# Sliding-window attention inside a fused layer stack: two transfers moved to the next step, and the softmax mask written by ScalarE

## The chip, the cores and the metric

The kernel runs on one core of a Trainium2 chip. The metric is the device time of one execution in microseconds (us), the median over several executions. The engines are named as in the profile: PE (TensorE, with its weight loads shown apart as PEld), DVE (VectorE), ACT (ScalarE), POOL (GpSimd) and SP (SyncE, which here only issues DMAs). All five run their own instruction streams and meet at counting semaphores.

## The reference

The input is x of shape (4, 1024, 128) in fp32. First comes a causal multi-head attention with low-rank projections and a layer norm. Then, and this is where the change lies, six layers of local attention and feed-forward, each on the whole of x:

```
for i in range(6):
    x = attn_layer(shift_tokens(x), Wqkv[i], q_scale[i], k_scale[i], Wo[i]) + x
    x = ffn_layer(shift_tokens(x), ln_g[i], ln_b[i], W1[i], b1[i], W2[i], b2[i]) + x
```

`attn_layer` projects to q, k and v of 16 heads of 64, normalises q and k per head, rotates them, and attends in windows of 32 tokens: a query sees its own window and the one before it, 64 keys, from which `(it < jb) | (it > jb + w) | (jb == -1)` are masked ahead of the softmax. The third condition masks the missing window before the first one. A last layer norm ends the computation.

## The kernel before

The program is written out in full: no loops at run time. The six layers are the function `local_layers`. It works in steps; a step takes a pair of token tiles, 256 tokens of one batch element, so there are 6 x 4 x 4 = 96 pairs, and 3 more steps drain the pipeline. In one step four pairs are in flight: `now` is projected to q, k and v, `back1` (the pair before) goes through scores, softmax and probabilities times V, `back2` through the output projection, `back3` through the feed-forward block. Each engine has a `step(s)` function in which its work stands in a fixed order, written by hand; there is no planner. PSUM holds three banks `bank_d` and three `bank_a`, each set used in turn through a `Ring`, and two banks `scores` for the attention scores of one phase.

The attention of a pair runs in two phases `ph` (even and odd windows) and within each in two halves (eight heads each, one score bank each):

- PE, `score(s, pair, ph, half)` (L457): first the mask as a matrix product of a bf16 identity with the bf16 mask (L465), which opens the bank; then 64 small matmuls q x k (L473) that accumulate on it. Phase 1 has first to wait until DVE has read phase 0's scores (`scores_used`). Phase 0 is ahead of projections 6, 7 and 8 (L410), phase 1 behind them.
- DVE, `softmax_shift` (L740): row maximum (L748), then the subtraction of it into `prob` (L752), each one instruction of 128x1024.
- ACT, `exponentials` (L643): the exponential in place (L645), behind the copy of v's first chunk (`copy_v(s, 8)`, L621) and the squares of q and k (`square`, L609).
- DVE, `softmax_sum`: row sum and reciprocal (L761, L762), in DVE's order ahead of the second phase's row maximum. POOL, `normalise`: the product with the reciprocal (L949).
- PE, `transpose_probs` (L420), then `times_v` (L440): 256 small matmuls and as many weight loads a step.

In the odd phase `times_v` takes its rows from `v`, in the even phase from `v_back`, which holds the same rows moved down by 32 tokens, over partition borders. SP makes it (L352 to L360), as soon as v's last chunk is copied, by three DMAs: 96 partitions of v's both tiles (768 KB), 32 partitions from tile 0 to tile 1 (128 KB), and the last 32 tokens of the *other* v buffer, the pair before (128 KB). Other things to know: ACT loads its function table twice a step, before the exponentials and before the gelu gates (L664); projection 9 on PE waits until the gates of part A have been read from their bank; PE's own instructions are brought in by DMA as well (queue q8 in the profile).

Of the kernel before, what the change touches and what calls it, by code (L numbers as in the profile page):

```python
# [21 lines left out]
P = 128  # L22
# [110 lines left out]
def local_layers(nc, x_dram, x1_dram, w):  # L133
# [5 lines left out]
    with ExitStack() as ctx:  # L139
# [76 lines left out]
        xr_in = [sem(f"xr_in{i}") for i in range(2)]  # L216
        xs1_in = [sem(f"xs1_in{i}") for i in range(2)]
        v_back_in = [sem(f"v_back_in{i}") for i in range(2)]
        x1_out, x2_out = sem("x1_out"), sem("x2_out")
        wqk_in, wv_in, wo_in, wffn_in, qkrow_in = sem("wqk_in"), sem("wv_in"), sem("wo_in"), sem("wffn_in"), sem("qkrow_in")  # L220
        d_filled, d_free = sem("d_filled"), sem("d_free")
# [3 lines left out]
        qk_ready = sem("qk_ready")  # L225
        table_ready = sem("table_ready")
        scores_ready, scores_used = sem("scores_ready"), sem("scores_used")
        exp_done, inv_ready, prob_ready = sem("exp_done"), sem("inv_ready"), sem("prob_ready")
        xn_ready = sem("xn_ready")
        v_link = sem("v_link")  # L230
# [44 lines left out]
        def _(sp):  # L275
# [40 lines left out]
            def step(s):  # L316
                new, now, back1, back2, back3 = (s.pair(lag) for lag in (-1, 0, 1, 2, 3))

                if not isinstance(s.t, int) or s.t > MAX_LAG:
                    sp.wait_ge(x2_out, 16 * (s.t - MAX_LAG))  # L320
                if runs(now):


                    load_xs(new)
                if runs(back2):


                    sp.dma_start(xr[back2.par][:, :, :], dram_rows(x_dram, back2.f, 1 + PAIR * back2.p, PAIR)
                                 .rearrange("(a t) d -> t a d", a=2)).then_inc(xr_in[back2.par], 16)
                if runs(now) and s.b == 0 and s.p == 0:  # L330
                    sp.wait_ge(table_ready, POS * (s.layer + 1))
                    load_qk_rows((s.layer + 1) % DEPTH)
                if runs(now) and s.b == BATCH - 1 and s.p == POS - 1:
                    sp.wait_ge(d_filled, chunk_at(now, 7)[1] + 1)
                    load_w_qkv((s.layer + 1) % DEPTH, 0, 2 * INNER, wqk_in)
                if runs(back2):
                    sp.wait_ge(d_free, ring_d.at(s, "y")[1] + 1)
                    sp.dma_start(x1_dram[1 + PAIR * back2.p:1 + PAIR * (back2.p + 1), :]
                                 .rearrange("(a t) d -> t a d", a=2), x1[back2.par][:, :, :]).then_inc(x1_out, 16)
                    sp.wait_ge(x1_out, 16 * (back2.n + 1))  # L340

                    if later(back2.n, 2):
                        sp.wait_ge(xn_ready, back2.n - 1)
                    row = 1 + PAIR * back2.p
                    for lo, hi, r in ((0, DIM // 2, row), (DIM // 2, DIM, row - 1)):
                        sp.dma_start(xs1[back2.par][:, :, lo:hi], x1_dram[r:r + PAIR, lo:hi]
                                     .rearrange("(a t) d -> t a d", a=2)).then_inc(xs1_in[back2.par], 16)
                if runs(back2) and s.b == 0 and s.p == 1 and in_rounds(s):

                    load_wo(s.layer)  # L350
                if runs(now):


                    sp.wait_ge(a_free, ring_a.at(s, (1, "v", 1))[1] + 1)
                    q = WINDOW
                    src, old, dst = v[now.par], v[1 - now.par], v_back[now.par]
                    done = v_back_in[now.par]
                    sp.dma_start(dst[q:P, :, :], src[0:P - q, :, :]).then_inc(done, 16)
                    sp.dma_start(dst[0:q, 1, :], src[P - q:P, 0, :]).then_inc(done, 16)
                    sp.dma_start(dst[0:q, 0, :], old[P - q:P, 1, :]).then_inc(done, 16)  # L360
                    if s.b == BATCH - 1 and s.p == POS - 1:

                        load_w_qkv((s.layer + 1) % DEPTH, 2 * INNER, 3 * INNER, wv_in)
                if runs(back3):
                    sp.wait_ge(d_free, ring_d.at(s, "y2")[1] + 1)
                    sp.dma_start(dram_rows(x_dram, back3.f + BATCH, 1 + PAIR * back3.p, PAIR)
                                 .rearrange("(a t) d -> t a d", a=2), x2[back3.par][:, :, :]).then_inc(x2_out, 16)
                    if s.b == 0 and s.p == 2 and in_rounds(s):

                        load_ffn(s.layer)  # L370
# [6 lines left out]
        def _(pe):  # L377
# [47 lines left out]
            def times_v(s, pair, half):  # L425


                if half == 0:
                    pe.wait_ge(v_back_in[pair.par], 48 * (pair.k + 1))
                banks = [fill_a(s, f"O{half}{u}", after="PT3") for u in range(2)]  # L430
                for j in range(4):
                    hp = 4 * half + j
                    for a in range(2):
                        for ph in range(2):
                            src = (v if ph else v_back)[pair.par]
                            col = P * j + 64 * a + 32 * ph
                            for u in range(2):
                                for h2 in range(2):
                                    h = 2 * hp + h2
                                    last = nc.tensor.matmul(  # L440
                                        banks[u][64 * h2:64 * h2 + 64, col:col + 32],
                                        src[64 * u:64 * u + 64, a, DH * h:DH * (h + 1)],
                                        probT[ph][64 * u:64 * u + 64, hp, 32 * (2 * h2 + a):32 * (2 * h2 + a) + 32],
                                        start=True, stop=True)
                last.then_inc(a_filled, 2)
# [10 lines left out]

            def score(s, pair, ph, half):  # L457
                pe.wait_ge(a_free, ring_a.at(s, f"qk{6 + half}")[1] + 1)
                if half == 0:
                    n = 2 * pair.n + ph  # L460
                    if later(n):
                        pe.wait_ge(scores_used, n)
                first = pair.p == 0 and ph == 0
                bank = scores[:, 4 * half:4 * half + 4, :, :]
                nc.tensor.matmul(bank, ident_b[:, :], mask[:, int(first), :, :, :], start=True, stop=False,  # L465
                                 skip_group_check=True)
                for hp in range(4 * half, 4 * half + 4):
                    for u in range(2):
                        for h2 in range(2):
# [47 lines left out]
                last.then_inc(a_filled, 1)  # L517

            pe.wait_ge(constants_ready, INIT)
            transpose_x(Step(-1, BATCH - 1, POS - 1))  # L520
            for i in range(EARLY):
                project(Step(-1, BATCH - 1, POS - 1), i)
# [70 lines left out]
        def _(act):  # L593
# [18 lines left out]
            def copy_v(s, i):  # L612
                now = s.pair(0)
                if not runs(now):
                    return
                a, _, c = chunks[i]
                bank = filled(s, chunks[i])
                if i == 8 and later(now.n):

                    act.wait_ge(v_back_in[1 - now.par], 48 * (prev(s).pair(0).k + 1))  # L620
                nc.scalar.activation(v[now.par][:, a, 512 * c:512 * (c + 1)], bank[:, :], ACT.Copy).then_inc(a_free, 1)  # L621

            def copy_x(s):
# [3 lines left out]
            def copy_qk(s, pair, i):  # L627
# [12 lines left out]
                                             scale=0.0 if pair.p == POS - 1 else 1.0)  # L640
                nc.scalar.activation(out, bank, ACT.Copy).then_inc(a_free, 1)

            def exponentials(pair, ph):  # L643
                act.wait_ge(scores_used, 2 * pair.n + ph + 1)
                nc.scalar.activation(prob[ph][:, :, :], prob[ph][:, :, :], ACT.Exp).then_inc(exp_done, 1)  # L645

            def copy_probs(s, ph):
# [20 lines left out]
            def step(s):  # L668
                new, now, back1, back2, back3 = (s.pair(lag) for lag in (-1, 0, 1, 2, 3))
                for i in range(4):  # L670
# [3 lines left out]
                    if i in (1, 3):  # L674
                        square(now, 4 + i // 2)
                square(now, 6)
                square(now, 7)
                copy_v(s, 8)
                if runs(back1):
                    exponentials(back1, 0)  # L680
# [21 lines left out]
                copy_v(s, 11)  # L702
                if new.exists:
                    copy_x(s)
                if runs(back3):
                    bank = filled(s, "y2T")
                    nc.scalar.activation(y2T[:, :], bank[:, 0:PAIR], ACT.Identity,
                                         bias=small[:, SMALL["b2"]:SMALL["b2"] + 1]).then_inc(a_free, 1)
# [9 lines left out]
                square(new, 3)  # L718

            act.wait_ge(constants_ready, INIT)  # L720
            copy_x(Step(-1, BATCH - 1, POS - 1))
            for i in range(EARLY):
                square(Step(-1, BATCH - 1, POS - 1).pair(-1), i)
# [4 lines left out]
        def _(dve):  # L728
# [13 lines left out]
            def softmax_shift(s, ph):  # L742
# [6 lines left out]
                if later(n, 2):  # L749

                    dve.wait_ge(a_filled, ring_a.at(prev(s), f"PT{2 * ph + 1}")[1] + 1)
                nc.vector.tensor_tensor(prob[ph][:, :, :], sc,  # L752
                                        row_max[:, ph, :].unsqueeze(2).to_broadcast([P, HEADS, 2 * WINDOW]),
                                        ALU.subtract).then_inc(scores_used, 1)

            def softmax_sum(s, ph):
                if not runs(s.pair(1)):
# [992 lines left out]
```

## Time and profile before

| | us |
|---|---|
| median of 3 runs | 4634.17 (4632.89 to 4639.07) |
| the profiled execution's own time | 4644.36 |
| its span | 4642.6 |
| PE busy | 4130.6 (89%) |
| DVE busy | 2893.4 (62%) |
| ACT busy | 2615.3 (56%) |
| POOL busy | 2707.4 (58%) |

Busy times are of the profiled execution. The first fifth of the span is the attention with low-rank projections; from about 960 us to about 4600 us run the 99 steps. The clock of TensorE has two levels, 2.4 and 1.2 GHz; the mean that was granted stands in the result as 0.95 of the full one. In rows of a timeline the first number is the start and the second the length, both in us, then engine, line, operation, the program's names (out<-in), shapes and how many instructions the row merges. In brackets stands how long the engine was idle before, and what released it: another engine's instruction, or "issue", where no semaphore that the profile knows held it.

### The profile page before, as it was taken

Reading aid. Unit: us, or ns where it says so; the run is one execution under the profiler, and the core shown is the slowest. Engines: PE = TensorE matmul, PEld = TensorE weight load, DVE = VectorE, ACT = ScalarE, POOL = GpSimd, SP = SyncE. Lnnn points to the kernel's source line nnn. Section 1 sums busy time; section 2 is a strip of 40 time slices with the busy share of each in tenths; the row PEclk is TensorE's granted clock in tenths of the full one; section 3 lists DMA queues with packets and bytes.
Section 4 is the critical chain, followed back from the end, with each engine's and each line's share of the span. In section 5 each row is a group of like instructions: output and inputs, shape, how many; then the busy total and the mean of one; then the engine's idle time right before and its main releaser. Section 6 shows DMA issues by size and latency. Waiting matters only on the chain. (4 is left out here: it accounts for less than half of the span.)

```text
span 4642.6 us, 152879 instructions
## 1 busy us (share of the span) xinstructions
PE 4130.6 (89%) x66876; PEld 2769.5 (60%) x66876; DVE 2893.4 (62%) x4211; ACT 2615.3 (56%) x4412; POOL 2707.4 (58%) x3440
## 2 busy tenths in 40 slices
PE   5879788679999999999999999999999999999994
PEld 2434344346666666666666666666666666666663
DVE  5565656456666666666666656666666666666664
ACT  2545353445555556666666655555656556666662
POOL 0000000067777777778777867677767777777781
PEclk9989898889999999999999999999999999999997
DMA  0000000111111211112211212111221112221122
GB/s 28 3 16 2 15 2 16 38 42 46 44 47 46 67 51 46 47 46 71 58 49 48 57 51 56 45 46 46 61 55 46 46 46 55 57 62 50 47 59 79
DMA packets 246285, 208.29 MB, mean 45 GB/s; under 512 B 118461, under 2 KB 227224, under 8 KB 235256
## 3 DMA queue, kind: packets, MB, share of 16 engines
q1 hardware_dynamic: 245624, 198.51, 16.3%
q8 instruction: 533, 8.73, 0.8%
q14 instruction: 128, 1.05, 0.1%
HBM read 68.01 MB, written 29.77 MB: 21 GB/s over the span
## 5 line engine op out<-in xcount | busy, mean ns | idle before, releaser
L782 DVE TENSOR_TENSOR products<-bank_d,table 128x1024 f32<-128x1024 f32 x768 | 933.1, 1215 | 861.8 <-ACT sq L609 840.9
L905 POOL TENSOR_TENSOR products<-products 128x2048 f32<-128x2048 f32 x192 | 871.8, 4541 | 458.4 <-DVE products L782 458.4
L410 PE MATMUL bank_d<-w_qkv,xT 128*128 128x512 f32 x1536 | 830.8, 656 | 14.4 <-issue 5.8
L609 ACT ACTIVATE sq<-bank_d 128x512 f32<-128x512 f32 x768 | 465.5, 606 | 449.9 <-PE bank_d L410 437.8
L942 POOL TENSOR_TENSOR qk_rot<-products,rnorm 128x2048 f32<-128x2048 f32 x192 | 695.7, 3624 | 7.6
L780 DVE TENSOR_REDUCE ss<-sq 128x16 f32<-128x1024 f32 x384 | 465.6, 1213 | 123.3 <-ACT sq L609 123.0
L869 POOL MEMSET ident<- 128x128 f32 x1 | 0.2, 205 | 911.0 <-POOLq L1060 911.0
L949 POOL TENSOR_TENSOR prob<-prob,inv_sum 128x1024 f32<-128x1024 f32 x192 | 365.4, 1903 | 250.7 <-DVE inv_sum L762 250.7
L1487 DVE TENSOR_REDUCE part_max<-s_max 128x1 f32<-128x512 f32 (+3 forms) x768 | 398.6, 554 | 150.7 <-PE s_max L1236 101.9
L440 PE MATMUL bank_a<-probT,v 64*64 64x32 f32 x12288 | 397.1, 222 | 60.4 <-issue 60.4
L656 ACT ACTIVATE attnT<-bank_a 128x512 f32<-128x512 f32 x384 | 208.4, 594 | 428.1 <-PE bank_a L440 428.1
L410 PE MATMUL bank_a<-w_qkv,xT 128*128 128x512 f32 x768 | 402.8, 607 | 51.9 <-ACT gate L664 50.1
L440 PE MATMUL bank_a<-probT,v_back 64*64 64x32 f32 x12288 | 396.0, 223 | 53.7 <-issue 50.3
L473 PEld LDWEIGHTS scores<-kT,qT 64*32 64x32 f32 x24576 | 361.0, 107 | 137.1 <-issue 137.1
L440 PEld LDWEIGHTS bank_a<-probT,v_back 64*64 64x64 f32 x12288 | 344.4, 137 | 162.0 <-issue 92.2
L1408 ACT ACTIVATE a_probT<-s_T 128x1024 f32<-128x1024 f32 x320 | 299.2, 938 | 248.4 <-PE s_T L1251 152.9
L473 PE MATMUL scores<-kT,qT 64*32 64x64 f32 x24576 | 424.0, 218 | 7.9 <-issue 7.9
L454 PEld LDWEIGHTS bank_a<-ident,qk_rot 128*128 128x128 f32 x3072 | 355.9, 145 | 75.9 <-issue 53.7
L454 PE MATMUL bank_a<-ident,qk_rot 128*128 128x128 f32 x3072 | 391.3, 281 | 7.2 <-POOL qk_rot L942 6.4
L440 PEld LDWEIGHTS bank_a<-probT,v 64*64 64x64 f32 x12288 | 349.4, 138 | 64.7 <-issue 64.7
L410 PEld LDWEIGHTS bank_d<-w_qkv,xT 128*128 128x128 f32 x1536 | 270.8, 202 | 194.8 <-issue 164.5
L487 PE MATMUL bank_a<-attnT,w_o 128*128 128x256 f32 x1536 | 351.9, 382 | 1.0 <-issue 0.9
(166 smaller groups left out, 7220.4 us busy)
## 6 DMA issues: line engine op xcount, KB each, us to landing
v_back<-v SPq DMA_DIRECT2D x96, 768.0 KB, 5.4
v_back<-v SPq DMA_DIRECT2D x192, 128.0 KB, 5.4
xs<-x_layers SPq DMA_DIRECT2D x194, 64.0 KB, 2.1
xr<-x_layers SPq DMA_DIRECT2D x96, 128.0 KB, 2.7
x<-x SPq DMA_DIRECT2D x96, 128.0 KB, 1.8
xs<-x SPq DMA_DIRECT2D x192, 64.0 KB
x_layers<-x SPq DMA_DIRECT2D x96, 128.0 KB, 1.8
w_qkv<-in_Wqkv_dram SPq DMA_DIRECT2D x7, 1024.0 KB, 5.1
```

The source lines that it names most:

```text
L410: nc.tensor.matmul(bank[:, :], xT[:, P * a:P * (a + 1)], w_qkv[:, col:col + 512], start=True, stop=True).then_inc(d_filled if i < 8 else a ...
L440: last = nc.tensor.matmul(banks[u][64 * h2:64 * h2 + 64, col:col + 32], src[64 * u:64 * u + 64, a, DH * h:DH * (h + 1)], probT[ph][64 * u: ...
L454: last = nc.tensor.transpose(bank[:, P * j:P * (j + 1)], qk_rot[:, a, col:col + P], ident[:, :])
L473: last = nc.tensor.matmul(scores[row:row + 32, hp, u, :], qT[64 * h2:64 * h2 + 64, hp, 32 * win:32 * win + 32], kT[pair.par][64 * h2:64 * ...
L487: last = nc.tensor.matmul(bank[:, 0:PAIR], w_o[:, hp, :], attnT[:, hp, :], start=(hp == 0), stop=(hp == HP - 1))
L609: nc.scalar.activation(sq[j % 2][:, 8 * c:8 * c + 8, :], bank_d[slot][:, :].rearrange("p (h d) -> p h d", d=DH), ACT.Square).then_inc(squa ...
L780: nc.vector.tensor_reduce(ss[:, a, HEADS * kq:HEADS * (kq + 1)], sq[i // 2 % 2][:, :, :], AX.X, ALU.add)
L782: nc.vector.tensor_tensor(products[:, a, head:head + 8, :, :].rearrange("p h r (o d) -> p h r o d", o=2), bank[:, :].rearrange("p (h r d) ...
L905: link(nc.gpsimd.tensor_tensor(products[:, a, :, 0, :], products[:, a, :, 0, :], products[:, a, :, 1, :], ALU.add))
L942: nc.gpsimd.tensor_tensor(qk_rot[:, a, :].rearrange("p (h d) -> p h d", d=DH), products[:, a, :, 0, :], rnorm[:, a, 0:2 * HEADS].unsqueeze ...
L949: nc.gpsimd.tensor_tensor(prob[ph][:, :, :], prob[ph][:, :, :], inv_sum[:, ph, :].unsqueeze(2).to_broadcast([P, HEADS, 2 * WINDOW]), ALU.m ...
L1487: nc.vector.tensor_reduce(part_max[:, head, col:col + 1], s_max[m % 2][:, 0:width], AX.X, ALU.max).then_inc(max_free, 1)
```

## The change

Three edits.

1. Of the three v_back transfers, the two that read the same pair's v are issued by SP one step later, once both phases' scores of that pair are computed (`scores_ready`). The third, from the other v buffer, stays where it was, and gets a semaphore of its own, `v_last_in`. PE waits for both kinds ahead of `times_v`.
2. The mask product on PE is gone. ACT writes the mask into each score bank by a Copy, `set_mask`, and PE's score matmuls accumulate on what ACT wrote (they have `start=False`). One product per bank at the start of the program opens the banks. The writes for the next pair's phase 0 stand behind `copy_x` in ACT's order; those for phase 1 ahead of and behind `square(now, 7)`.
3. DVE's subtraction is two instructions of 128x512, one per score bank, each with its own increment of `scores_used`.

```diff
@@ SP, step
+                if runs(back1):
+                    sp.wait_ge(scores_ready, 2 * back1.n + 2)
+                    src, dst, done = v[back1.par], v_back[back1.par], v_back_in[back1.par]
+                    sp.dma_start(dst[WINDOW:P, :, :], src[0:P - WINDOW, :, :]).then_inc(done, 16)
+                    sp.dma_start(dst[0:WINDOW, 1, :], src[P - WINDOW:P, 0, :]).then_inc(done, 16)
                 if runs(back2):
                     sp.wait_ge(d_free, ring_d.at(s, "y")[1] + 1)
...
                     sp.wait_ge(a_free, ring_a.at(s, (1, "v", 1))[1] + 1)
-                    q = WINDOW
-                    src, old, dst = v[now.par], v[1 - now.par], v_back[now.par]
-                    done = v_back_in[now.par]
-                    sp.dma_start(dst[q:P, :, :], src[0:P - q, :, :]).then_inc(done, 16)
-                    sp.dma_start(dst[0:q, 1, :], src[P - q:P, 0, :]).then_inc(done, 16)
-                    sp.dma_start(dst[0:q, 0, :], old[P - q:P, 1, :]).then_inc(done, 16)
+                    sp.dma_start(v_back[now.par][0:WINDOW, 0, :], v[1 - now.par][P - WINDOW:P, 1, :]).then_inc(
+                        v_last_in[now.par], 16)
@@ PE, times_v and score
-                    pe.wait_ge(v_back_in[pair.par], 48 * (pair.k + 1))
+                    pe.wait_ge(v_last_in[pair.par], 16 * (pair.k + 1))
+                    pe.wait_ge(v_back_in[pair.par], 32 * (pair.k + 1))
...
-                if half == 0:
-                    n = 2 * pair.n + ph
-                    if later(n):
-                        pe.wait_ge(scores_used, n)
-                first = pair.p == 0 and ph == 0
-                bank = scores[:, 4 * half:4 * half + 4, :, :]
-                nc.tensor.matmul(bank, ident_b[:, :], mask[:, int(first), :, :, :], start=True, stop=False,
-                                 skip_group_check=True)
+                pe.wait_ge(mask_set, 2 * (2 * pair.n + ph) + half + 1)
@@ PE, once at the start
+            for half in range(2):
+                opened = nc.tensor.matmul(scores[:, 4 * half:4 * half + 4, :, :], ident_b[:, :], mask[:, 0, :, :, :],
+                                          start=True, stop=True)
+            opened.then_inc(scores_opened, 1)
@@ ACT
+            def set_mask(pair, ph, half):
+                if not runs(pair):
+                    return
+                n = 2 * pair.n + ph
+                if later(n):
+                    act.wait_ge(scores_used, 2 * (n - 1) + half + 1)
+                first = int(pair.p == 0 and ph == 0)
+                nc.scalar.activation(scores[:, 4 * half:4 * half + 4, :, :], mask[:, first, :, :, :],
+                                     ACT.Copy).then_inc(mask_set, 1)
...
                 square(now, 6)
+                set_mask(back1, 1, 0)
                 square(now, 7)
+                set_mask(back1, 1, 1)
                 copy_v(s, 8)
...
                     copy_x(s)
+                set_mask(now, 0, 0)
+                set_mask(now, 0, 1)
@@ DVE, softmax_shift
-                nc.vector.tensor_tensor(prob[ph][:, :, :], sc,
-                                        row_max[:, ph, :].unsqueeze(2).to_broadcast([P, HEADS, 2 * WINDOW]),
-                                        ALU.subtract).then_inc(scores_used, 1)
+                for half in range(2):
+                    hu = slice(HEADS // 2 * half, HEADS // 2 * (half + 1))
+                    nc.vector.tensor_tensor(prob[ph][:, hu, :], sc[:, hu, :],
+                                            row_max[:, ph, hu].unsqueeze(2).to_broadcast([P, HEADS // 2, 2 * WINDOW]),
+                                            ALU.subtract).then_inc(scores_used, 1)
```

ACT's wait of `exponentials` counts the new increments, and its wait ahead of `copy_v(s, 8)` is now for `v_last_in`.

## Rows read from the trace of the kernel before

**Rows 1.** The page: busy time by engine; granted clock in 40 slices, in tenths.

```profile
PE 4130.6 (89%) x66876; PEld 2769.5 (60%) x66876; DVE 2893.4 (62%) x4211; ACT 2615.3 (56%) x4412; POOL 2707.4 (58%) x3440
...
PEclk9989898889999999999999999999999999999997
```

**Rows 2.** Timeline of SP: the store of x1, issued once per step.

```profile
1022.57 0.37 SPq L338 DMA_DIRECT2D x<-x  x1
...
2445.01 0.37 SPq L338 DMA_DIRECT2D x<-x  x1
...
2480.24 0.37 SPq L338 DMA_DIRECT2D x<-x  x1
...
4522.17 0.37 SPq L338 DMA_DIRECT2D x<-x  x1
```

**Rows 3.** Windows: stretch, length, busy by engine (instructions), granted clock, DMA share, GB/s.

```profile
2162.00:2338.00 176.00, 170.86 (x3144) 120.85 (x3143) 119.42 (x143) 114.45 (x204) 137.42 (x176) 1.00 0.22 57
...
2945.00:3145.00 200.00, 186.21 (x3231) 130.45 (x3229) 122.13 (x147) 117.26 (x209) 140.47 (x182) 0.94 0.19 48
```

**Rows 4.** Waits of the whole span: us in total, times, longest.

```profile
PE bank_a L440 <- issue: 110.7, 67, 4.7
```

**Rows 5.** Timelines of PE and SP around pauses, and in a quiet step.

```profile
2449.70 1.98 PE L410 MATMUL bank_d<-w_qkv,xT 128*128 128x512 f32 x4
...
2612.48 0.41 PE L473 MATMUL scores<-kT,qT 64*32 64x64 f32 x12 [1.33 <-issue]
...
3140.90 2.03 SPq L360 DMA_DIRECT2D v_back<-v  x1
...
3146.47 0.24 PE L440 MATMUL bank_a<-probT,v 64*64 64x32 f32 x2 [1.58 <-issue]
...
3147.44 3.58 PE L410 MATMUL bank_d<-w_qkv,xT 128*128 128x512 f32 x4
```

**Rows 6.** The page: a DMA queue (packets, MB, share); a DMA group (to landing, us).

```profile
q8 instruction: 533, 8.73, 0.8%
...
v_back<-v SPq DMA_DIRECT2D x96, 768.0 KB, 5.4
```

**Rows 7.** Timeline of PE in the quiet step.

```profile
2430.26 1.02 PE L410 MATMUL bank_a<-w_qkv,xT 128*128 128x512 f32 x2
2431.57 0.38 PE L465 MATMUL scores<-mask,ident_b 128*128 128x512 bf16 x1 [0.28 <-DVE prob L752]
...
2433.23 1.10 PE L473 MATMUL scores<-kT,qT 64*32 64x64 f32 x64
...
2441.89 1.12 PE L410 MATMUL bank_a<-w_qkv,xT 128*128 128x512 f32 x2 [0.54 <-ACT gate L664]
...
2444.36 1.04 PE L420 MATMUL bank_a<-ident,prob 128*128 128x128 f32 x8
```

**Rows 8.** Timeline of ACT in the quiet step.

```profile
2431.94 1.28 ACT L645 ACT_TABLE_LOAD   x1
2433.23 1.06 ACT L645 ACTIVATE prob<-prob 128x1024 f32<-128x1024 f32 x1
...
2438.35 0.38 ACT L689 ACTIVATE yT<-bank_a 128x256 f32<-128x256 f32 x1 [2.89 <-PE bank_a L487]
2438.63 1.05 ACT L645 ACTIVATE prob<-prob 128x1024 f32<-128x1024 f32 x1
...
2449.84 1.08 ACT L656 ACTIVATE attnT<-bank_a 128x512 f32<-128x512 f32 x2 [1.55 <-PE bank_a L440]
```

**Rows 9.** Timeline of DVE in the quiet step.

```profile
2430.20 1.23 DVE L752 TENSOR_TENSOR prob<-scores,row_max 128x1024 f32<-128x1024 f32 x1
...
2434.32 1.22 DVE L761 TENSOR_REDUCE row_sum<-prob 128x16 f32<-128x1024 f32 x1 [1.77 <-ACT prob L645]
...
2436.94 1.22 DVE L752 TENSOR_TENSOR prob<-scores,row_max 128x1024 f32<-128x1024 f32 x1
```

**Rows 10.** Timeline of POOL in the quiet step.

```profile
2441.92 1.90 POOL L949 TENSOR_TENSOR prob<-prob,inv_sum 128x1024 f32<-128x1024 f32 x1 [0.52 <-DVE inv_sum L762]
```

More of the change, by code:

```diff
@@ L218, in local_layers @@
         v_back_in = [sem(f"v_back_in{i}") for i in range(2)]
+        v_last_in = [sem(f"v_last_in{i}") for i in range(2)]
         x1_out, x2_out = sem("x1_out"), sem("x2_out")
@@ L227, in local_layers @@
         scores_ready, scores_used = sem("scores_ready"), sem("scores_used")
+        mask_set = sem("mask_set")
+        scores_opened = sem("scores_opened")
         exp_done, inv_ready, prob_ready = sem("exp_done"), sem("inv_ready"), sem("prob_ready")
@@ L618, in copy_v @@
                 if i == 8 and later(now.n):
-                    act.wait_ge(v_back_in[1 - now.par], 48 * (prev(s).pair(0).k + 1))
+                    act.wait_ge(v_last_in[1 - now.par], 16 * (prev(s).pair(0).k + 1))
                 nc.scalar.activation(v[now.par][:, a, 512 * c:512 * (c + 1)], bank[:, :], ACT.Copy).then_inc(a_free, 1)
@@ L641, in copy_qk @@
                 nc.scalar.activation(out, bank, ACT.Copy).then_inc(a_free, 1)
+            def set_mask(pair, ph, half):
[7 more added lines that the diff above has]
+                                     ACT.Copy).then_inc(mask_set, 1)
             def exponentials(pair, ph):
-                act.wait_ge(scores_used, 2 * pair.n + ph + 1)
+                act.wait_ge(scores_used, 2 * (2 * pair.n + ph) + 2)
                 nc.scalar.activation(prob[ph][:, :, :], prob[ph][:, :, :], ACT.Exp).then_inc(exp_done, 1)
@@ L720, in _ @@
             act.wait_ge(constants_ready, INIT)
+            act.wait_ge(scores_opened, 1)
             copy_x(Step(-1, BATCH - 1, POS - 1))
```

## The prediction, made before the changed kernel was run

> **What bounds the kernel now.** I read the slices of the page first, then SP's timeline for the pace of the steps, the windows of two stretches, the waits, and one step engine by engine. TensorE is busy in nine tenths of the span and its granted clock lies between 0.8 and 1 of full [rows 1]. The 96 window-attention steps have a clean pace: SP's store of x1 (L338) is issued once per step. The first stands at 1022.57, the last before the draining steps at 4522.17 [rows 2], with 92 issues between, so 93 intervals in 3499.6 us, 37.63 us each. Two neighbours in a quiet stretch stand 35.23 us apart [rows 2]. So the kernel has a quiet step of 35.23 us, and on average loses 2.40 us to something else: 93 x 2.40 = 223 us.
>
> What it loses is seen in two windows. From 2162 to 2338 the clock is granted in full (2.4 GHz) and PE is busy 170.86 of 176 us; from 2945 to 3145 the clock is 0.94 of it and PE is busy 186.21 of 200 [rows 3]. The waits name it: 67 times TensorE stood in the probs-times-V matmuls (L440) "on issue", 110.7 us together, 1.65 us each, 4.7 at most [rows 4]; no semaphore holds it. One such place: SP issues the last v_back transfer at 3140.90 (it takes SP 2.03 us); TensorE stops inside L440 for 1.58 us until 3146.47; the four projections behind it then take 3.58 us, where in a quiet step the same four take 1.98 [rows 5]: the lower level (1.2 GHz) of the clock for a while, 1.6 us more. Queue q8 carries the instructions: 533 packets, 8.73 MB, so 16 KB each [rows 6]. TensorE has 66876 matmuls and as many weight loads in this program, 133752 instructions; divided by 533 that is 251 a packet. L440 has 256 matmuls and 256 loads a step in a few us, so two packets have to come in there, just when SP has put 768 KB, and with the two small ones 1 MB, into the DMA engines; it lands a median 5.4 us after issue [rows 6]. I read the pauses as instruction packets held up behind v_back.
>
> In the quiet step the end is set by PE, with two short holds: 0.28 us at the mask product of the second score phase, for DVE's subtraction, and 0.54 us at projection 9 (L410 at 2441.89), for the gelu gate [rows 7]. From 2441.89 to the same point of the next step PE runs without a break worth naming. So what moves those two places moves the step.
>
> **Part 1: v_back's large transfers.** They are issued one step later, after both score phases (scores_ready), not during L440. In the step shown the second phase's last matmuls run from 2433.23 [rows 7], so that is about 2434. SP has nothing to do from its small loads to its next store at 2445.01 [rows 2], so no queue entry is held up by the new wait; the weight loads that share the place come once per layer. With 0.54 + 0.6 us of issue and 5.4 to landing the rows are there by about 2441; L440's first half lies ahead of the projections at 2449.70 [rows 5], from about 2447.7. That is 6 us of cover; if it went, L440 would wait for what is missing. Between 2434 and 2447 PE runs few, wide matmuls (w_o, FFN, two transposes), so a packet of instructions that is late there is not missed. The 128 KB from the older v stay where they were. What goes: the pauses in L440 and the clock they cost, all 223 us but a rest. The rest: pauses that v_back has no part in, such as 1.33 us inside the scores at 2612.48 [rows 5], and those beside weight loads at the layer ends (the 4.7 us one). PE's timeline has nine such of 0.75 us and more, these two among them, 20 us together. Bounds: none goes (0), all goes (223).
>
> **Part 2: the mask.** PE loses four products of 0.38 us, 0.31 between starts, 1.24 us a step. I book nothing for it: the first phase's two are cut ahead of DVE, which doesn't wait for scores there (its max starts when its product ends), and the second phase is decided by ACT, below.
>
> ACT gains four writes of 128x512. None is in the trace; nearest are copies of 128x512 from a bank, two of which take 1.08 us, so 0.49 from start to start and 0.59 for the last [rows 8]. Lower bound: the 128x256 copy, 0.38; upper: the exponential of 128x1024, 1.06 [rows 8]. I take 0.49 to 0.59, because size and type of the output are the same. The two for the next first phase come after copy_x; ACT waits 1.55 us for PE ahead of attnT [rows 8], which hides them: 0.
>
> The two for the second phase don't hide. ACT is in order, and set_mask(1, half 0) stands ahead of square 7 and waits for DVE's subtraction. Today the subtraction runs 2430.20 to 2431.43 [rows 9]; its first half, now an instruction of its own, would end at about 2430.85 (half of 1.23 and a few hundredths; the pair costs DVE 0.07 more). Queued behind this wait: square 7, the second mask, copy_v 8, the table load, the first exponential. ACT then runs: mask 2430.9, square 7 at 2431.4, mask 2431.9, copy_v 2432.4 to 2433.0, table load 1.28 [rows 8], exponential at about 2434.3. Today it starts at 2433.23 [rows 8]: 1.07 us late. PE gets the second phase's masks at 2431.5 and 2432.5, scores until 2433.7: no later than today, but it now stands idle for 0.9 us after projection 8 (it ends today at 2431.28 [rows 7], without the first two masks at 2430.66).
>
> **Where the lateness ends.** DVE already waits 1.77 us for that exponential [rows 9], so all 1.07 us go on: sum, reciprocal, second max, second subtraction. That one starts today at 2436.94 and would end at 2439.31 with the 0.07. The second exponential starts today at 2438.63, because yT (2438.35) comes ahead of it [rows 8]; 0.47 us of slack after the subtraction's end at 2438.16 swallow part. It would start at 2439.36: 0.73 late. Then table load and gate, and PE's projection 9 at 2442.62, not 2441.89. Check of the other branch: second sum after the exponential, ends 2442.7; POOL's normalisation starts at 2443.1 (today 2441.92, 1.90 long [rows 10]), ends 2445.0; PE wants it at 2444.36 [rows 7] + 0.73 = 2445.09. It just fits.
>
> So the quiet step becomes 35.23 + 0.73 = 35.96 us, though PE has 1.24 us less to do. Bounds of this term: writes of 0.38 give +0.33, writes of 1.06 give +1.9 (4618 in all); PE's gain alone would be -1.24. The Trainium skill (ScalarE: Activation LUTs, Step-by-step: what each stage is for) says ScalarE reaches PSUM sooner than SBUF; no row here has such a write. With it the term would lean to its lower end, about 4472 in all.
>
> **Sum**, against the profiled execution's own 4644.36 us (span 4642.6; 0.22% above the median of 4634.17): 4644.4 - 223.2 + 93 x 0.73 (67.9) + 20 = 4509 us. The changed kernel should hardly have the spread that pauses give, so I don't take the 10 us to the median off. That is 2.7% below the median.
>
> **Rivals.**
> C, packets locked to a bad place. A step has today some five packets and a few instructions, which is why quiet and noisy stretches alternate. Eight instructions go (four masks, four loads), a few waits come; the remainder comes near zero, so packets come at one place of the step for long. If that is at the head of a dense block, PE pauses in every step, v_back or no v_back. For it: the 1.33 us in the scores [rows 5]. Against: such pauses are rare today. At 0.8 us a step: 4509 + 74 = 4583.
> A, the clock. PE now stands twice in a step, 0.9 us ahead of the second scores and 0.54 + 0.73 = 1.27 us ahead of projection 9. If the clock falls to 1.2 GHz after one of them in every step, it costs the 1.6 us of [rows 5]: 4509 + 149 = 4658, slower. It decides from 1.45 us a step (135 / 93). For it: it fell after the pause of 1.58 us. Against: after that of 1.33 us at 2612.48 the next work runs at its usual pace, and the two new pauses are shorter still.
> B, the pauses aren't v_back's. Then they stay and ACT's lateness is added: 4644 + 68 = 4712, slower. For it: pauses exist away from v_back. Against: 67 in L440, few elsewhere, and the quiet steps run the same L440 without one. The Trainium skill speaks for B (Runtime: NRT & Kernel Launch, Instruction fetch mechanics): the engine streams its program in 16 KiB blocks and crossing a block's border is "mostly hidden"; it gives TensorE room for eight blocks. The size agrees with rows 6; that it is hidden, the 110.7 us of rows 4 don't bear out.
>
> **Chances.** Forecast 0.66 (own range 4455 to 4560), C 0.17, A 0.09, B 0.08. Below 4455 little is left: every pause gone and masks at nothing is 4421. Range 4450 to 4615: it holds the forecast, C and all but the last of the ACT term's upper bound, and leaves out A and B. A measurement here can tell 0.2%, some 9 us. Faster 0.84, within 0.2% 0.03 (A at half strength), slower 0.13.
>
> **What would show it.** Right: "issue" ahead of L440 falls from 110.7 to under 30 us; L338 comes every 35.9 to 36.2 us nearly everywhere; ACT's first exponential comes about 1 us later after projection 8's copy; PE's idle before projection 9 grows to about 1.3 us, before the second scores to about 0.9, now released by ACT; clock at 1.00. Wrong: pauses in every step at one place (C); four projections at 3.58 us in steady steps (A); L440 pausing as before (B); or DVE's wait for the exponential below 2.3 us, which would make the ACT term too large.

## The result, and the profile after

The changed kernel takes 4532.28 us (median of 4 runs, 4529.81 to 4536.63), the kernel before 4633.64 beside it. The ratio is 0.978, 95% interval 0.9763 to 0.9797: faster. Forecast were 4509, range 4450 to 4615. Two executions, one of e3 (6742 us) and one of e6 (11660 us), stand far above all others of their kernels and are left out of every time below.

The page of the changed kernel: span, busy time by engine, granted clock by slice, two DMA groups.

```profile
span 4528.0 us, 152979 instructions
PE 3935.5 (87%) x66494; PEld 2686.2 (59%) x66494; DVE 2887.8 (64%) x4403; ACT 2788.6 (62%) x4796; POOL 2702.7 (60%) x3440
...
PEclk9979797979999999999999999999999999999997
...
v_back<-v SPq DMA_DIRECT2D x96, 768.0 KB, 5.3
v_back<-v SPq DMA_DIRECT2D x192, 128.0 KB, 5.1
```

Three readings against [rows 1] and [rows 6]. The slices of the clock are too coarse to show the change: from the tenth on they read 9 in both pages. ACT is busy for 173 us more, but the kernel is faster: busy shares say nothing here. The two transfers are no faster than before; they are somewhere else.

SP's timeline: the store of x1, once per step (L347 now), as in [rows 2].

```profile
1026.80 0.38 SPq L347 DMA_DIRECT2D x<-x  x1
...
2433.86 0.54 SPq L343 DMA_DIRECT2D v_back<-v  x1
2434.44 1.48 SPq L344 DMA_DIRECT2D v_back<-v  x1
2445.80 0.38 SPq L347 DMA_DIRECT2D x<-x  x1
...
2881.71 0.38 SPq L347 DMA_DIRECT2D x<-x  x1
2917.71 0.38 SPq L347 DMA_DIRECT2D x<-x  x1
...
4412.00 0.38 SPq L347 DMA_DIRECT2D x<-x  x1
```

The stores at 2881.71 and 2917.71 give the quiet step: 36.00 us. First and last are again 93 steps apart: 3385.2 us, 36.40 each, where it was 37.63. The rest of the span has not moved: 4528.0 - 3385.2 = 1142.8, before 4642.6 - 3499.6 = 1143.0. So all of the gain is in the steps, 93 x 1.23 = 114 us between these two executions: the quiet step grew by 0.77, and what is lost beside it fell from 2.40 to 0.40. Between the same two stores the trace has TensorE "on issue" for 125 us before and 34 us after, and its clock granted at 1.2 GHz for 174 us in 38 stretches before and for 14 us in 4 after. As an estimate, the pauses and half of the time at 1.2 GHz make 212 of the 223 us before.

The waits of PE "on issue" in the changed kernel (us in total, times, longest), as in [rows 4], and a window, as in [rows 3]:

```profile
PE bank_a L446 <- issue: 20.4, 27, 1.4
PE scores L472 <- issue: 10.7, 9, 1.8
PE bank_a L494 <- issue: 4.7, 3, 2.0
...
2900.00:3100.00 200.00, 182.36 (x3325) 131.31 (x3325) 133.60 (x173) 137.98 (x248) 153.77 (x197) 1.00 0.20 51
```

From 110.7 us to 20.4 at the probs-times-V matmuls, and the full clock (2.4 GHz) with three holds in every step (below: at L472, L494 and L415).

One quiet step, ACT first, then PE. By chance it stands at nearly the same time as the quiet step of before (its y2 product 0.03 us later), so starts can be compared directly with [rows 7 to 9].

```profile
2428.97 0.60 ACT L612 ACTIVATE sq<-bank_d 128x512 f32<-128x512 f32 x1 [2.29 <-PE bank_d L415]
2430.95 0.60 ACT L654 ACTIVATE scores<-mask 128x512 f32<-128x512 bf16 x1 [1.39 <-DVE prob L773]
2431.49 0.58 ACT L612 ACTIVATE sq<-bank_d 128x512 f32<-128x512 f32 x1
2431.97 0.59 ACT L654 ACTIVATE scores<-mask 128x512 f32<-128x512 bf16 x1
2432.49 0.59 ACT L624 ACTIVATE v<-bank_a 128x512 f32<-128x512 f32 x1
2433.09 1.28 ACT L659 ACT_TABLE_LOAD   x1
2434.39 1.06 ACT L659 ACTIVATE prob<-prob 128x1024 f32<-128x1024 f32 x1
...
2439.42 1.06 ACT L659 ACTIVATE prob<-prob 128x1024 f32<-128x1024 f32 x1 [0.69 <-DVE prob L773]
...
2447.84 1.12 ACT L654 ACTIVATE scores<-mask 128x512 f32<-128x512 bf16 x2
```

```profile
2431.70 2.10 PE L472 MATMUL scores<-kT,qT 64*32 64x64 f32 x128 [1.05 <-ACT scores L654]
2434.42 0.44 PE L494 MATMUL bank_a<-ident,xn 128*128 128x128 f32 x2 [0.61 <-POOL xn L954]
...
2442.68 1.13 PE L415 MATMUL bank_a<-w_qkv,xT 128*128 128x512 f32 x2 [1.27 <-ACT gate L678]
...
2445.15 1.04 PE L425 MATMUL bank_a<-ident,prob 128*128 128x128 f32 x8
```

The rows show the queue: mask, square, mask, v copy, table load, exponential, without a gap, all behind one wait for DVE. The exponential starts 1.16 us later than in [rows 8], projection 9 0.79 later than in [rows 7].

### The profile page after: what moved, and what is told of

It reads as the page before. It is cut to its first block and busy times, and to the rows that moved or that the text cites. A ratio compares the mean times of both kernels' runs of the same rounds, so it can differ in the third digit from the quotient of the medians.

```text
span 4528.0 us, 152979 instructions
## 1 busy us (share of the span) xinstructions
PE 3935.5 (87%) x66494; PEld 2686.2 (59%) x66494; DVE 2887.8 (64%) x4403; ACT 2788.6 (62%) x4796; POOL 2702.7 (60%) x3440
## 5 line engine op out<-in xcount | busy, mean ns | idle before, releaser
L415 PE MATMUL bank_d<-w_qkv,xT 128*128 128x512 f32 x1536 | 775.4, 617 | 4.9 <-DVE products L803 3.5
L472 PEld LDWEIGHTS scores<-kT,qT 64*32 64x32 f32 x24576 | 363.6, 107 | 266.3 <-issue 189.7
L415 PE MATMUL bank_a<-w_qkv,xT 128*128 128x512 f32 x768 | 403.6, 608 | 112.3 <-ACT gate L678 110.5
L472 PE MATMUL scores<-kT,qT 64*32 64x64 f32 x24576 | 397.7, 217 | 111.8 <-ACT scores L654 101.0
L782 DVE TENSOR_REDUCE row_sum<-prob 128x16 f32<-128x1024 f32 x192 | 233.2, 1215 | 273.4 <-ACT prob L659 273.4
L446 PEld LDWEIGHTS bank_a<-probT,v_back 64*64 64x64 f32 x12288 | 329.1, 134 | 111.8 <-ACT attnT L670 70.8
L446 PE MATMUL bank_a<-probT,v 64*64 64x32 f32 x12288 | 377.5, 219 | 16.3 <-issue 16.3
L460 PEld LDWEIGHTS bank_a<-ident,qk_rot 128*128 128x128 f32 x3072 | 342.4, 141 | 74.8 <-issue 51.7
L460 PE MATMUL bank_a<-ident,qk_rot 128*128 128x128 f32 x3072 | 380.5, 276 | 7.0 <-POOL qk_rot L963 6.6
L446 PE MATMUL bank_a<-probT,v_back 64*64 64x32 f32 x12288 | 377.1, 220 | 7.4 <-issue 4.1
L415 PEld LDWEIGHTS bank_d<-w_qkv,xT 128*128 128x128 f32 x1536 | 255.8, 191 | 167.6 <-issue 141.1
```

What stands on the lines that cost most here:

```text
L415: nc.tensor.matmul(bank[:, :], xT[:, P * a:P * (a + 1)], w_qkv[:, col:col + 512], start=True, stop=True).then_inc(d_filled if i < 8 else a ...
L446: last = nc.tensor.matmul(banks[u][64 * h2:64 * h2 + 64, col:col + 32], src[64 * u:64 * u + 64, a, DH * h:DH * (h + 1)], probT[ph][64 * u: ...
L460: last = nc.tensor.transpose(bank[:, P * j:P * (j + 1)], qk_rot[:, a, col:col + P], ident[:, :])
L472: last = nc.tensor.matmul(scores[row:row + 32, hp, u, :], qT[64 * h2:64 * h2 + 64, hp, 32 * win:32 * win + 32], kT[pair.par][64 * h2:64 * ...
```

## The experiments

All times are medians of four to six executions beside the kernel before, which took 4625 to 4630 us; of each run the ratio's 95% interval is given. "Lost" is the mean step less the quiet step, both from SP's stores.

**1. Edit 1 alone, and edits 2 and 3 alone.**

```diff
 e1_back_only: kernel before, and
+                    sp.wait_ge(scores_ready, 2 * back1.n + 2)   # the two large transfers here
...
 e2_mask_only: changed kernel, and
-                    sp.wait_ge(scores_ready, 2 * back1.n + 2)   # they stand again behind v's last copy
```

> Only edit 1: the two large v_back transfers one step later; mask product and one subtraction as before. Theory (two independent effects: the transfers cause most pauses, the mask by ScalarE costs 0.7 to 0.8 us a step): quiet step 35.2 us, pauses left about 0.4 us a step as in the changed kernel, so 93 x 35.65 + 1143 + 2, about 4460 us. Rival (the pauses went because the program has another length or ScalarE's wait shifts TensorE, not because of the transfers): pauses stay, 4634 us.

> Only edits 2 and 3: mask by ScalarE, subtraction in two; all v_back transfers as before. Theory: quiet step 36.0 us and the pauses in the probs-times-V matmuls back, 1 to 3 us in about two steps of three; 4634 + 93 x 0.77, about 4700 us. Since TensorE's order has more slack now, 4670 is possible. Rival (the mask itself pays and the transfers are hidden anyway): 4530 us.

Measured: e1 4469.61 us, ratio 0.9643 (0.9623 to 0.9664); e2 4695.10 us, ratio 1.0128 (1.0099 to 1.0156). Waits of PE in e1, then in e2:

```profile
PE bank_a L444 <- issue: 22.7, 28, 1.6
```

```profile
PE bank_a L443 <- issue: 117.8, 64, 5.6
```

The transfers decide about the pauses, with the mask product or without it. In e1 0.57 us a step are lost beside a quiet step of 35.20, where 0.40 were expected. The mask by ACT is a loss of 65 us by itself, the transfers a gain of 161; 0.9643 x 1.0128 = 0.9766, where both together measured 0.978. Within these intervals the two edits don't act on each other.

**2. The transfer as such.** The changed kernel with added transfers to a buffer that nobody reads.

```diff
 e5_dummy_load: behind the small v_back transfer
+                        sp.wait_ge(extra_in, 16 * s.t)   # the step before's; 32 in e10
+                    sp.dma_start(extra[WINDOW:P, :, :], v[now.par][0:P - WINDOW, :, :]).then_inc(extra_in, 16)
 e10_dummy_full: the same, and, both ahead of the small v_back transfer
+                    sp.dma_start(extra[0:WINDOW, 1, :], v[now.par][P - WINDOW:P, 0, :]).then_inc(extra_in, 16)
```

> The changed kernel with one more transfer of 768 KB per step, from v to a buffer that nobody reads, issued where the large v_back transfer stood in the kernel before. Everything else is as in the changed kernel, also the waits of TensorE. Theory (what stops TensorE is that transfer beside its instruction packets): pauses ahead of the probs-times-V matmuls back to over 90 us in all, 4620 to 4700 us. Rival (TensorE paused for another reason, for instance its wait for v_back_in): 4530 us.

> As the run e5_dummy_load, but with both large transfers of the kernel before doubled at their old place (768 and 128 KB to a buffer that nobody reads) and issued in the old order, ahead of the small one that stayed. In e5 the pauses ahead of the probs-times-V matmuls came back only in part, 44.1 us in place of 20.4, where the kernel with all v_back transfers at the old place has 117.8. Theory (order and amount of what the instruction packets meet): pauses 80 us or more, 4650 to 4700 us. Rival (the extra bytes matter little; what is needed is that TensorE's own buffer is the target, or that v_back is missing from the other place): 40 to 55 us of pauses, 4590 us.

Measured: e5 4589.01 us, 0.9914 (0.9892 to 0.9937); e10 4681.61 us, 1.011 (1.0088 to 1.0132). The waits, e5 and e10:

```profile
PE bank_a L451 <- issue: 44.1, 33, 3.9
```

```profile
PE bank_a L452 <- issue: 114.5, 65, 4.8
```

e5 missed its forecast: a quarter of the pauses at the probs-times-V matmuls came back (44.1 us, between 20.4 and e2's 117.8), and 57 us of time. e10 has nearly all of them, and is within 14 us of e2. No compute engine waits for these bytes (SP alone does, one step later), so TensorE can't be waiting for data: their presence at that time stops it. How much of the step from e5 to e10 is the 128 KB and how much the order on the queue was not told apart.

That it is the instruction packets which are held up stands in the traces, if all of TensorE's instructions are counted through (matmuls, weight loads and waits). Before, these are 136240 for 533 packets of q8, 255.6 each. Within a trace, a pause "on issue" of over 0.5 us always comes at the same remainder of the count divided by 256, so at a packet's border (where the instructions of the next packet begin), and it ends 1.1 to 1.8 us after a packet of q8 has landed. The last two columns take the borders for which the border before lies in the probs-times-V matmuls too (256 instructions, 3.84 us without a pause): how many there are, and how long after the border before the next packet's transfer starts (median).

| | pauses from 1000 us on | remainder | borders with a pause | borders without |
|---|---|---|---|---|
| before | 77 | 59 or 60 | 51, packet starts after 3.2 us | 39, after 0.7 us |
| changed | 31 | 59 or 60 | 9, after 2.2 us | 82, after 0.8 us |
| e10 | 76 | 246 or 247 | 49, after 3.3 us | 42, after 0.7 us |
| e7 (part 4) | 8 | 246 or 247 | 7, after 2.6 us | 88, after 0.8 us |

The packet itself takes a median 1.0 to 1.3 us in all of them. (Which remainder it is depends only on where the trace's count begins. In e1 it moves by 4 a step, because the four mask products of a step are missing from its trace, where their weight loads stand.) In the example of [rows 5] the border before is passed at 3140.82, the packet starts at 3143.88 and lands at 3145.10, and TensorE goes on at 3146.47.

**3. What the mask costs: place or time.**

```diff
 e3_masks_last
                 square(now, 6)
-                set_mask(back1, 1, 0)
                 square(now, 7)
-                set_mask(back1, 1, 1)
                 copy_v(s, 8)
+                set_mask(back1, 1, 0)
+                set_mask(back1, 1, 1)
 e6_whole_sub: one subtraction of 128x1024, which counts scores_used up by 2
```

> The changed kernel with both of phase 1's mask writes behind copy_v 8 in ScalarE's order, not around square 7. Theory (what costs is that square 7, a mask and copy_v 8 queue behind DVE's subtraction, not the writes): first exponential 0.7 to 0.8 us earlier, quiet step 35.2 to 35.35 us, about 4460 us. Rival (what costs is ScalarE's time for the writes, 2 x 0.5 us ahead of the exponential wherever they stand): quiet step stays 35.9 to 36.0, 4530 us.

> The changed kernel with the subtraction as one instruction of 128x1024. Theory (chain subtraction, mask, square 7, mask, copy_v 8, exponential): the first mask write starts 0.55 to 0.6 us later; of that 0.6 less the 0.07 that the single instruction saves arrives at projection 9: quiet step 36.5 us, about 4575 us. Rival (ScalarE's own time for the writes is what counts): no change, 4530 us.

Measured: e3 4472.24 us, 0.9654 (0.9633 to 0.9675); e6 4586.52 us, 0.9919 (0.9896 to 0.9943). The v copy of the kernel before; then ACT in e3, where the wait for the subtraction is gone; then in e6:

```profile
2431.32 0.60 ACT L621 ACTIVATE v<-bank_a 128x512 f32<-128x512 f32 x1 [0.26 <-PE bank_a L410]
```

```profile
2509.99 0.60 ACT L624 ACTIVATE v<-bank_a 128x512 f32<-128x512 f32 x1 [0.26 <-PE bank_a L415]
2510.49 1.11 ACT L654 ACTIVATE scores<-mask 128x512 f32<-128x512 bf16 x2
2511.61 1.28 ACT L659 ACT_TABLE_LOAD   x1
2512.91 1.06 ACT L659 ACTIVATE prob<-prob 128x1024 f32<-128x1024 f32 x1
...
2517.70 0.38 ACT L705 ACTIVATE yT<-bank_a 128x256 f32<-128x256 f32 x1 [2.89 <-PE bank_a L486]
2517.99 1.05 ACT L659 ACTIVATE prob<-prob 128x1024 f32<-128x1024 f32 x1
```

```profile
2522.35 0.60 ACT L654 ACTIVATE scores<-mask 128x512 f32<-128x512 bf16 x1 [1.98 <-DVE prob L771]
...
2530.81 1.06 ACT L659 ACTIVATE prob<-prob 128x1024 f32<-128x1024 f32 x1 [1.24 <-DVE prob L771]
```

In e3 the same two writes stand where ACT has to wait for nobody; the quiet step is 35.23 us, as before the change, and the run is 60 us below the changed kernel. So what costs 0.77 us is their place behind a wait, with square 7 and the v copy behind it. The writes are not free for all that. Set side by side at yT (2438.35 in [rows 8], 2517.70 here), the two writes put 1.1 us ahead of the table load, but projection 8 and with it the v copy come 0.68 us earlier, since the mask products are gone from PE. The first exponential is 0.33 us late, and the second starts right behind yT as before: the slack there takes the 0.33. e6 turns the same screw the other way: ACT's wait grows from 1.39 to 1.98, the quiet step to 36.58. Without edit 3 the change would have gained less than half as much.

**4. The pauses that are left.** Counting TensorE's instructions in the trace from step to step gives 1275 before, 1270 after and in e3, e5, e6, e8 and e10 (1269 in e2), against 5 x 256 = 1280 for five packets. So the border of a packet moved by 5 instructions a step before and by 10 after. In the changed kernel slow steps stand in groups about 26 steps apart (256 / 10): those with pauses at L446 begin at 1356, 2264, 3248 and 4195 us, those at the scores at 1813, 2716 and 3669. The kernel before is quiet from 2021 to 2659 us and again from 4063 on, 54 steps from begin to begin (256 / 5 = 51).

```diff
+                if s.t >= 4:
+                    for _ in range(10):    # e4_pad10; 20 in e7_pad20
+                        pe.wait_ge(constants_ready, INIT)
                 project_now(9)
```

> The changed kernel with ten more waits per step on TensorE that are fulfilled long before (ahead of projection 9, where it idles 1.27 us). A step has 1270 instructions of TensorE in the trace; with ten more it has 1280, five packets of 256. Theory (the pauses left come where a packet's border lies in a dense block): the border stays at one quiet place, pauses of ordinary steps vanish, only layer ends stay; quiet step 36.0, 4528 - 30, about 4500 us. Rival (the pauses left have nothing to do with the border): 4532, or 4560 if the border stays at a bad place.

> The changed kernel with twenty fulfilled waits per step on TensorE ahead of projection 9. In the run with ten, TensorE's instructions in the trace were 1275 a step, since two waits go into one instruction; with twenty they should be 1280, five packets of 256. Theory (packet borders in dense blocks cause the pauses left): the border stays at a place that was quiet in the run with ten, ordinary steps have no pause, about 4502 us (36.05 a step, 10 to 15 us for layer ends). Rival: pauses go on as before, 4540 us.

Measured: e4 4541.30 us, 0.9798 (0.9778 to 0.9819); e7 4506.36 us, 0.9741 (0.972 to 0.9761). e4 failed by my count: ten waits made five instructions, the step had 1275 and the border went on wandering, at half the pace. It had slow groups of up to eight steps where the changed kernel has three or four, and lost 0.54 us a step where that one lost 0.40. In e7 the step has 1280 and keeps its border. Its waits:

```profile
PE bank_a L446 <- issue: 8.9, 7, 1.9
...
PE scores L472 <- issue: 2.0, 2, 1.5
```

Lost falls from 0.40 to 0.10 us a step (36.16 against 36.06); the five steps over 36.5 us all stand at a layer's end, where the next layer's weights are loaded (1.5 MB for the projections alone). Five runs lie between 4504.84 and 4508.00.

The expectation puts the pauses down to borders in dense blocks, which is too simple. In e7 two borders of every ordinary step lie inside L446 (at 2435.03 and 2438.87, for instance), at nearly the same place in the block as the pause at 3146.47 of the kernel before, and TensorE passes them: the packet of the second one starts at 2435.72 and lands at 2437.03. So a border in a dense block makes a pause only where the packet is late as well; what still makes some packets late in the changed kernel (after 2.2 us instead of 0.8) was not tested. The 128 KB of v_back that stayed there are a candidate.

**5. A version that beats both.** In the quiet step the end is set by the chain DVE, ACT, DVE, ACT, PE through both exponentials, and ACT loads its table in that chain although it had 1.39 us of idle time just before.

```diff
 e8_early_exp (ACT's order)
                 square(now, 6)
+                nc.scalar.activation(warm[:, :], ident[:, 0:1], ACT.Exp)
                 set_mask(back1, 1, 0)
-                square(now, 7)
                 set_mask(back1, 1, 1)
+                exponentials(back1, 0)
+                square(now, 7)
                 copy_v(s, 8)
-                exponentials(back1, 0)
...
+                exponentials(back1, 1)
                 bank = filled(s, "yT")
...
-                exponentials(back1, 1)
 e9_both: the same with the twenty waits of e7
```

> The changed kernel with another order on ScalarE: after square 6 one exponential of a single column, so that the function table is loaded while ScalarE waits for DVE; then both masks, the first exponential, square 7, copy_v 8; and the second exponential ahead of yT. Theory (TensorE's hold of 1.27 us at projection 9 is the end of the chain through both exponentials): first exponential 2.2 us earlier, the hold goes, quiet step 36.0 - 1.27, about 34.7 us, 4410 us in all. Rival (chain through TensorE, DVE or GpSimd takes over sooner): 35.2 us, 4460.

> ScalarE's order of the run e8_early_exp and the twenty fulfilled waits of the run e7_pad20 together. In e8 the quiet step was 34.40 us and the pauses cost some 70 us over the run; the waits cost 0.06 us a step in e7. Theory (the two are independent): 93 x 34.46 + 1143 + 12 for layer ends, about 4361 us. Rival (with less slack on TensorE the packet border at this place isn't quiet any more, or the waits now cost their full time): 4400 us or more.

Measured: e8 4411.87 us, 0.9533 (0.9512 to 0.9553); e9 4347.35 us, 0.9398 (0.937 to 0.9426). ACT and then PE in a quiet step of e8:

```profile
2518.69 1.28 ACT L693 ACT_TABLE_LOAD   x1
2519.98 0.20 ACT L693 ACTIVATE warm<-ident 128x1 f32<-128x1 f32 x1
2520.09 1.17 ACT L655 ACTIVATE scores<-mask 128x512 f32<-128x512 bf16 x2
2521.19 1.04 ACT L660 ACTIVATE prob<-prob 128x1024 f32<-128x1024 f32 x1
```

```profile
2520.82 1.99 PE L473 MATMUL scores<-kT,qT 64*32 64x64 f32 x128 [1.07 <-ACT scores L655]
2523.54 0.44 PE L495 MATMUL bank_a<-ident,xn 128*128 128x128 f32 x2 [0.73 <-POOL xn L957]
...
2530.30 1.02 PE L416 MATMUL bank_a<-w_qkv,xT 128*128 128x512 f32 x2
```

The hold at projection 9 is gone, the quiet step is 34.40 us. The two holds ahead of it stay (ACT's mask and POOL's xn). e8 moves the table load, the first and the second exponential at once; what each is worth by itself was not measured, and the step became 0.33 us shorter than the hold of 1.27 explains. e9 came out 14 us below its forecast: the twenty waits cost nothing here (its quiet step is 34.40 too), which is 6 us of them; the rest is within the spread of its runs (4344.68 to 4354.82).

## Why the prediction was right, and where it was off

- **The pace and its two parts** held: a quiet step and pauses laid upon it. Sum of the steps 93 x 35.96 + 20 = 3364 forecast, 3385 measured in the profiled run.
- **Pauses from v_back**: right in cause (e1, e2, e10, and the packets of part 2) and nearly in size. With TensorE's waits counted a packet has 255.6 instructions, not 251. Taken: all 223 us but 20. Left over: 93 x 0.40 = 37 us.
- **The term that was mis-sized** is this rest of 20 us. It was counted from nine pauses before (they add up to 19.4 us), as if those at L440 could only be v_back's. The trace of after shows ones of 0.4 to 1.4 us at L446 with the large transfers elsewhere. By e7, 9 of the 37 us belong to layer ends (93 x 0.10), the other 28 go with the wandering of the packet border. These 17 us are most of the 21 us by which the profiled execution exceeds the forecast.
- **Part 2, the queue on ACT**: right step for step. Forecast and measured starts: first mask 2430.9 and 2430.95, exponential 2434.3 and 2434.39, second exponential 2439.36 and 2439.42, projection 9 2442.62 and 2442.68. The write was taken at 0.49 to 0.59 and is 0.60, with 0.52 to 0.54 to the next start. The quiet step came out 0.77 longer, not 0.73: 93 x 0.04 = 4 us.
- **Nothing booked for the masks taken off PE**: right for this order of ACT, where PE reaches the second phase 0.6 us earlier and holds 1.05 us for it (forecast 0.9). In e3 the same 0.6 us are what pays for more than half of the two writes. A third hold, 0.61 us ahead of L494 for POOL, was not foreseen; it lies between the other two and doesn't lengthen the step.
- **Cover of the moved transfers**: they are issued at 2433.86 (forecast about 2434), and no wait for v_back appears among PE's.
- **Rival A, the clock**: refuted. Holds of 1.05, 0.61 and 1.27 us per step leave the clock at 1.00 from 2900 to 3100.
- **Rival B**: refuted by e1 and by e10. The Trainium skill (Runtime: NRT & Kernel Launch, Instruction fetch mechanics) says that an engine fetches its program in 16 KiB blocks, that crossing their border is "mostly hidden", and that TensorE has room for eight. The size agrees: all pauses counted come at one remainder of 256, and 1280 instructions a step keep the border. That it is hidden agrees where the packet starts in time (88 borders in e7's L446), not with v_back beside it (51 pauses before). Room for eight doesn't agree: a packet that starts 3.2 us after one border is already missed at the next.
- **Rival C**: it did not come about, and its premise was wrong. I put the step's count near 1280 after the change; it went from 1275 to 1270, away from it, so the border wandered faster. Held on purpose (e7) at one place, which was quiet, it pays 26 us; no run held it at a bad one, so what C would have cost stays open.
- **What the two errors did not touch**: the direction and the ratio, 0.973 forecast, 0.978 measured.

## What to carry to other kernels

When an engine stops "on issue" in a block of many small instructions, look at which large transfer runs beside its instruction packets; moving that transfer to a stretch of few, wide instructions was worth 161 us here, and nobody had waited for its data. An operation taken off the busiest engine and given to an idle one costs by its place in that engine's order: two writes of 0.6 us cost 0.77 us a step behind a wait and ahead of a square and a copy, and nothing behind these two, where the time won on the busy engine and a slack further on paid for them. Before sizing such a move, follow the chain through the engine that is not busy, and count the instructions of a step: their remainder to a packet decides at which places of the step a late packet is missed.

## What the runs showed of the hardware that was not expected

- Ten fulfilled waits on one semaphore became five instructions in TensorE's stream (1270 to 1275 a step), twenty became ten (1280). In e9 they cost no time that can be seen; in e7 0.06 us a step.
- ScalarE writing 128x512 fp32 into a score bank from bf16 in SBUF takes 0.60 us, as its copies of the same size out of a bank into SBUF do (means 0.595 to 0.599 for v, probT and attnT). The Trainium skill (ScalarE: Activation LUTs, Step-by-step: what each stage is for) says that ScalarE reaches PSUM sooner than SBUF; the length of the row doesn't show it, and no run has the same copy into SBUF beside it.
- A subtraction of 128x512 takes 0.69 us on VectorE, where 128x1024 takes 1.22; two of them in a row 1.29 together, 0.07 more than the one.
- 768 KB beside the dense block brought a quarter of the pauses back, the same with 128 KB more and ahead of the small transfer nearly all of them (44.1 and 114.5 us, against 20.4 and 117.8).
- Every long pause "on issue" in the steps (77 before, 31 in the changed kernel) comes at one and the same remainder of TensorE's instruction count divided by 256, and ends 1.1 to 1.8 us after an instruction packet has landed.
